# Graph layers on one core: edge passes by pairs of groups, with VectorE instructions of 1024 columns

## The reference

```python
for l in range(5):                                     # block 1, edge_attr_32
    h = leaky(x @ W1[l] + b1[l]) @ W2[l] + b2[l]
    e = leaky(edge_attr @ We1[l] + be1[l]) @ We2[l] + be2[l]
    msg = h[src] * e * dot_scale[l]
    agg = segment_sum(msg, dst, num_segments=n)
    x = layernorm(x + agg * res_w[l]) * ln_g[l] + ln_b[l]
# block 2: rst = segment_sum((features * deg_out**-0.5 @ weight)[src], dst) * deg_in**-0.5 + bias
# block 3: two transformer convolutions with a softmax over each target's edges
# block 4, edge_attr_64:
msgs = relu(node_inputs[src] + edge_inputs)
return node_inputs + segment_sum(msgs, dst, num_segments=n)
```

## Time and profile before

| | us |
|---|---|
| median of 3 runs | 7263.68 |
| the profiled execution | 7279.41 |
| its span | 7277.8 |
| PE busy | 5581.7 (77%) |
| VectorE (DVE) busy | 5235.6 (72%) |
| ScalarE (ACT) busy | 2933.9 (40%) |
| GpSimd (POOL) busy | 3154.9 (43%) |
| mean granted TensorE clock | 0.877 |

### The profile page before, as it was taken

The page is one execution under the profiler, slowest core; times in us unless marked ns, Lnnn a source line. Parts: engine busy times, 40 slices in busy tenths (PEclk is TensorE's granted clock), DMA queues, the critical chain, the costliest instruction groups (busy, mean ns, idle before and its releaser), DMA issues. The chain is left out here.

```text
span 7277.8 us, 277545 instructions
## 1 busy us (share of the span) xinstructions
PE 5581.7 (77%) x87504; PEld 4594.4 (63%) x87511; DVE 5235.6 (72%) x14769; ACT 2933.9 (40%) x5054; POOL 3154.9 (43%) x4856
## 2 busy tenths in 40 slices
PE   4888888855555467777777777776889998999777
PEld 3666666633444357677677677676857776777676
DVE  7555555568999968888788788788955554555698
ACT  2444444423444534334344343343833332333343
POOL 1777767648777535445355354453000000000254
PEclk9989889975555579999899899898969998999999
DMA  2666666632222368778688587685631111111497
GB/s 73 195 190 189 187 179 191 184 104 63 73 72 74 125 195 230 191 192 230 154 229 231 154 229 208 173 230 159 244 114 61 62 64 47 64 64 64 113 237 202
DMA packets 1403295, 1098.83 MB, mean 151 GB/s; under 512 B 1012405, under 2 KB 1171820, under 8 KB 1393466
## 3 DMA queue, kind: packets, MB, share of 16 engines
q1 hardware_dynamic: 787494, 772.05, 34.5%
q0 software_dynamic: 224768, 240.90, 13.7%
q10 hardware_dynamic: 390804, 82.65, 6.2%
HBM read 815.28 MB, written 278.78 MB: 150 GB/s over the span
## 5 line engine op out<-in xcount | busy, mean ns | idle before, releaser
L542 POOL DMA_DIRECT2D big<-rows x2592 | 1421.8, 549 | 3245.3 <-issue 2301.5
L1316 PE MATMUL ps<-big 128*128 128x64 bf16 x41472 | 1922.4, 194 | 619.4 <-DVE big L1818 223.7
L1316 PEld LDWEIGHTS ps<-big 128*128 128x128 fp8e4 x41472 | 1688.1, 98 | 698.5 <-issue 686.1
L1328 PE MATMUL ps<-big 128*128 128x64 bf16 x20736 | 1734.1, 194 | 11.2 <-issue 5.8
L811 POOL DMA_INDIRECT rows<-big x800 | 1038.1, 1298 | 529.0 <-issue 356.9
L1328 PEld LDWEIGHTS ps<-big 128*128 128x128 bf16 x20736 | 1069.9, 98 | 21.7 <-issue 13.8
L1607 DVE SCALAR_TENSOR_TENSOR big<-big 128x1000 f32<-128x1000 f32 (+1 forms) x300 | 359.6, 1199 | 664.2 <-ACT big L917 438.0
L1037 ACT CAST big<-big 128x512 bf16<-128x512 f32 x720 | 445.4, 619 | 902.2 <-DVE big L1831 901.4
L1276 PE MATMUL ps<-identb,big 128*128 128x128 bf16 x2304 | 441.8, 294 | 395.4 <-DVE big L1719 300.3
L1231 PEld LDWEIGHTS ps<-big 128*125 128x125 f32 (+1 forms) x4800 | 678.1, 210 | 101.1 <-issue 57.9
L1043 ACT CAST big<-big 128x512 bf16<-128x512 f32 x864 | 534.0, 618 | 455.8 <-issue 336.3
(11 more groups left out here) (264 smaller groups left out, 9442.8 us busy)
## 6 DMA issues: line engine op xcount, KB each, us to landing
big<-ohsD SPq DMA_DIRECT2D x432, 512.0 KB, 3.8
big<-ohdD SPq DMA_DIRECT2D x432, 320.0 KB, 4.3
big<-rows POOLq DMA_DIRECT2D x2592, 32.0 KB, 3.8
big<-rows SPq DMA_DIRECT2D x2592, 32.0 KB, 3.6
big<-maskD SPq DMA_DIRECT2D x50, 1600.0 KB, 6.7
big<-rows ACTq DMA_DIRECT2D x1728, 32.0 KB, 3.6
big<-keyT SPq DMA_DIRECT2D x100, 488.3 KB
maskD<-big SPq DMA_DIRECT2D x25, 1600.0 KB, 6.2
```

What stands on the lines that cost most here:

```text
L542: eng.dma_start(edge[:, s.r, j, :], rows[bass.ds(v[s.r * (hi - lo) + j - lo], P), col]).then_inc(landed[s.r], 16)
L1316: last = pe.matmul(pG[g.r][:, j * D:(j + 1) * D], ohsR[:, g.r, at:at + P].bitcast(F8), slices[:, g.r, q, (3 * k + c) * D:(3 * k + c + 1) * D],
L1328: last = pe.matmul(pacc[:, bass.ds(w[j], D)], hot[:, g.r, j * P:(j + 1) * P], parts[:, g.r, c, j * D:(j + 1) * D], start=False, stop=False ...
```

## The change

- Edge passes work on pairs of groups (`Pair` in place of `Step`, 72 pairs); the loop body holds four pairs (`PR`), that is 8 groups, and the rings are 8 groups deep.
- `message`, `rest` and `lower` are single instructions of 1024 columns. The parts are kept as f32, and TensorE and `rest`/`lower` read the upper two bytes of each f32 as a bf16 (`upper_half`, a view with a step of two elements). ScalarE's casts `upper` and `middle` go; in block 4 it applies the relu to the message in f32.
- The target one-hots are neither stored nor loaded; VectorE remakes all of them (`remake`, 2048 columns per pair) from the local ids. Four tiles' one-hots are interleaved (`[d, j]` with the tile innermost), against an iota that is spread four times (`iota4`). TensorE reads them with a step of four elements.
- In the counting stretch VectorE makes the source one-hots of four tiles in one instruction, two per group, and the target one-hots of all eight in one.
- ScalarE copies the table slices, and waits for the whole split of the table first. The shares of the edge tiles are 4 (SyncE), 3 (GpSimd) and 1 (ScalarE).

```diff
-G_LAG, S_LAG = 1, 5
 RING = 4
+PR = 4
+NPAIR = NG // 2
+PT = NPAIR // PR
+S_LAG = 3
...
+        iota4 = sb("iota4", [P, 2 * P, QUAD], BF16)
...
-        slices = carve(RING, 2, 6 * D, dt=BF16)
-        ohsR = carve(RING, 2 * GT * P, dt=U8)
-        edge = carve(RING, GT, D)
+        slices = carve(2 * PR, 2, 6 * D, dt=BF16)
+        ohsR = carve(2 * PR, 2 * GT * P, dt=U8)
+        edge = carve(2 * PR, GT, D)
...
-        SP_SHARE, POOL_SHARE, ACT_SHARE = (0, 3), (3, 6), (6, 8)
+        SP_SHARE, POOL_SHARE, ACT_SHARE = (0, 4), (4, 7), (7, 8)
...
+        def upper_half(v):
+            return v.bitcast(BF16).rearrange("p (a b) -> p a b", b=2)[:, :, 1]
...
+            def load_hots(u):
+                sp.dma_start(ohsR[:, 2 * u.r:2 * u.r + 2, :], ohsD[bass.ds(u.i * 2, 2)].rearrange("g p f -> p g f")).then_inc(ohs_loaded[u.r], 16)
...
+                def step(u):
+                    if u.r == 0:
                         hold(sp)
+                        v[:] = starts(SP, u.t, *SP_SHARE, 2 * PR)
+                    if u.live(PR):
+                        sp.wait_ge(m_ready, base + u.lag(PR).i + 1)
                         hold(sp)
+                    load_hots(u)
+                    load_edges(sp, v, u, *SP_SHARE, col, edge_loaded)
...
                 act.copy(tabp[1], tres).then_inc(tab_mid, 1)
+                act.wait_ge(tab_mid, nth + 1)
+                act.wait_ge(tab_lo, nth + 1)
+
+            def slice_tables(u, names):
+                for k in range(4):
+                    last = act.copy(slices[:, 2 * u.r + k // 2, k % 2, :], flat(tabq)[:, bass.ds(names[u.r * 4 + k], 6 * D)])
+                last.then_inc(sliced, 1)
...
+            def edge_pass(base, positive, col):
+                v = list(starts(SCALAR, 0, *ACT_SHARE, 2 * PR))
+                for r in range(PR):
+                    load_edges(act, v, Pair(0, r), *ACT_SHARE, col, edge_loaded)
+                names = list(tables_of(SCALAR, 0))
...
+            def scatter(u, k, j, at):
+                own = hot[:, u.r, (k * 2 + j // QUAD) * QUAD * P:(k * 2 + j // QUAD + 1) * QUAD * P].rearrange("p (d j) -> p j d", j=QUAD)
                 for c in range(3):
+                    f = k * GT * D + j * D
+                    last = pe.matmul(pacc[:, bass.ds(at, D)], own[:, j % QUAD, :], upper_half(part(u, c)[:, f:f + D]),
                                      start=False, stop=False, skip_group_check=True)
...
+            def turn_over(u, v, base, nth):
+                to = u.lag(S_LAG)
+                if u.live(S_LAG):
+                    pe.wait_ge(lo_ready, base + to.i + 1)
...
+                hold(pe)
+                w = halves(v[u.r * GT:(u.r + 1) * GT], (W - 1) * D) if u.live(S_LAG) else ()
...
+            def same(to, local, groups):
+                n = groups * GT // QUAD
+                return dve.tensor_tensor(to.rearrange("p (q d j) -> p q d j", q=n, j=QUAD),
+                                         iota4[:, 0:P, :].unsqueeze(1).to_broadcast([P, n, P, QUAD]),
+                                         local.rearrange("p (q j) -> p q j", j=QUAD).unsqueeze(2).to_broadcast([P, n, P, QUAD]), ALU.is_equal)
...
+            def src_hots(t, r, q):
+                dve.tensor_tensor(ohS[:, r % 2, q * QUAD * 2 * P:(q + 1) * QUAD * 2 * P].rearrange("p (i j) -> p i j", j=QUAD), iota4[:, :, :],
+                                  each(idm[:, r % 2, q * QUAD:(q + 1) * QUAD], 2 * P), ALU.is_equal).then_inc(hots_ready, 1)
...
                     if not past(i, NG - 1) or not isinstance(i, int):
-                        one_hots(*chunk(t, r, 1), m)
+                        if m == 0:
+                            dst_hots(*chunk(t, r, 1))
+                        if m in (1, QUAD):
+                            src_hots(*chunk(t, r, 1), m // QUAD)
...
+            def rest(u, base, kind):
+                if u.live():
...
+                    dve.tensor_tensor(part(u, 1), part(u, 0), upper_half(part(u, 0)), ALU.subtract).then_inc(res_ready, 1)
+
+            def lower(u, base):
+                if u.live(1):
+                    g = u.lag(1)
+                    dve.wait_ge(res_ready, base + g.i + 1)
+                    dve.tensor_tensor(part(g, 2), part(g, 1), upper_half(part(g, 1)), ALU.subtract).then_inc(lo_ready, 1)
+
+            def all_pairs(base, kind, nth):
+                def body(u):
+                    message(u, base, kind, nth)
+                    lower(u, base)
+                    remake(u)
+                    rest(u, base, kind)
+                steps(dve, body)
```

More of the change, by code:

```diff
@@ L728, in _ @@
+                    load_hots(u)
+                    load_edges(sp, v, u, *SP_SHARE, col, edge_loaded)
+                for r in range(PR):
+                    step(Pair(0, r))
+                with sp.Fori(1, PT) as t:
+                    for r in range(PR):
+                        step(Pair(t, r))
             with sp.Fori(0, LAYERS) as l:
@@ L1302, in open_sums, with gather @@
                     pe.matmul(bank(b), zerob[:, :], zerob[:, 0:1].to_broadcast([P, 512]), start=True, stop=False, skip_group_check=True)
[L1304 to L1314 removed]
+            def gather(u, k, j):
+                g, q = u.r * 2 + k, j // QUAD
+                for half in range(2):
+                    at = ((q * 2 + half) * QUAD + j % QUAD) * P
@@ L1326, in scatter @@
-            def scatter(g, j, w):
+                        last = pe.matmul(pG[g % 4][:, j * D:(j + 1) * D], ohsR[:, g, at:at + P].bitcast(F8),
+                                         slices[:, g, q, (3 * half + c) * D:(3 * half + c + 1) * D],
+                                         start=(half + c == 0), stop=(half + c == 3))
+                return last
+            def scatter(u, k, j, at):
+                own = hot[:, u.r, (k * 2 + j // QUAD) * QUAD * P:(k * 2 + j // QUAD + 1) * QUAD * P].rearrange("p (d j) -> p j d", j=QUAD)
@@ L1806, in _ @@
-            names = []
-            def slice_tables(s, base):
-                if s.live(0):
-                    if s.r == 0:
-                        hold(dve)
-                        names[:] = tables_of(DVE, s.t)
-                    if not s.known or s.i >= RING:
-                        dve.wait_ge(gathered, base + s.lag(RING).i + 1)
-                        hold(dve)
-                    for q in range(2):
-                        last = dve.tensor_copy(slices[:, s.r, q, :], flat(tabq)[:, bass.ds(names[s.r * 2 + q], 6 * D)])
-                    last.then_inc(sliced, 1)
@@ L1837, in rest, with remake @@
-            def rest(s, base, kind):
-                if s.live(3):
-                    g = s.lag(3)
-                    dve.wait_ge(hi_ready, base + g.i + 1)
-                    if not g.known or g.i >= 2:
-                        dve.wait_ge(lo_ready, base + g.lag(2).i + 1)
+                        dve.tensor_tensor(part(u, 0), got, own, ALU.mult).then_inc(m_ready, 1)
+                    else:
+                        dve.tensor_tensor(part(u, 1), got, own, ALU.add).then_inc(m_ready, 1)
+            def remake(u):
+                if u.live():
+                    same(hot[:, u.r, :], dstl[:, bass.ds(u.i * 2 * GT, 2 * GT)], 2)
@@ L1874, in _ @@
                 table_parts(l)
-                def body(s):
-                    slice_tables(s, l * NG)
-                    message(s, l * NG, "edge", l)
-                    rest(s, l * NG, "edge")
-                    lower(s, l * NG)
-                    remake(s, l * NG)
-                steps(dve, body)
+                all_pairs(l * NPAIR, "edge", l)
                 lc = Chain(dve, l_chain, l * END)
@@ L1895, in _ @@
             barrier(dve, "L0")
-            def plain_pass(base, kind):
-                def body(s):
-                    slice_tables(s, base)
-                    message(s, base, kind, LAYERS)
-                    rest(s, base, kind)
-                    lower(s, base)
-                    remake(s, base)
-                steps(dve, body)
             chain(dve.tensor_tensor(t2, x, over(deg[:, 0, :], D), ALU.mult))
```

355 lines of the change are left out of this document (124 added, 231 removed).

## The result

Seven runs of each kernel, taken in turn: 7317.93 us after (7306.15 to 7350.97), 7269.26 before (7249.06 to 7294.06). The ratio is 1.0084, with a 95% interval of 1.0065 to 1.0102: the change costs 47 to 74 us. The forecast was a gain of 15. The time lies inside the range of 7125 to 7510 that was given, on the other side of no change from the forecast, and 8 us above the 7190 to 7310 that belonged to the forecast itself. The profiled run of after took 7350.97 us, its span is 7349.4.

A forecast was written before the change was run, and what follows sets the result against it. SyncE's DMA issuing was taken to bound the edge passes. Edge passes -101, counting stretch +83 and spreading the iota +3 sum to -15 us, forecast 7249 us against the median of 7263.68, range 7125 to 7510.

The forecast's parts named there:

- the sum of the edge passes: Five layer passes 14 us earlier each, 70 us, and the last 31: -101 us, with bounds -200 and -10.
- the body of 8 groups: Edge passes: SyncE issues 8 groups in 23.45 us, 2.93 per group against 2.98; bounds 2.81 to 3.04.
- What bounds the passes: Layers' edge passes: SyncE's DMA issuing is the bound, its queue 98% full; DVE and PE wait for what it issues late.
- The start: Start of an edge pass: SyncE resumes 14.9 us after the table split, with 8 groups loaded ahead and not 4.
- The end: End of an edge pass: landing 3.7, late gather 0.4, DVE 5.9, PE 4.4 us, 14.4 until the sums are read.
- The last pass: Final edge pass: bodies of 21.8 us, sums read at 7225.7 against 7257.4, 31 us earlier.
- The wait that was to show it: Edge passes: the sign expected in the profile was DVE idle before the message, released by a DMA of rows.
- rival (a): Wide comparisons on DVE run at a column per cycle: 230 us more in counting, 20 in passes, time 7500; chance 0.12.
- rival (b): PE's strided reads in the edge passes are slow, 6.9 us a pair: +455 us, 7700; chance 0.12.
- rival (c): PE's longer loop body is fetched again at each of 102 returns: +255 us, 7505; chance 0.06.
- rival (d): Reading 32 values is nearly free and the counting stretch's small waits go: -200+63 us, 7127; chance 0.2.
- The counting stretch: Three 1024-column one-hots per group overrun gaps between dependent adds: 6.55 us a group against 5.97, +83 us; bounds +60, +310.

The follow-up runs named there:

- e1_pieces: The changed kernel with the counting stretch's one-hots cut into 8 pieces of 340 to 512 columns, one behind each add: 7203.71 us, ratio 0.9908 to the kernel before.

## Why the prediction was wrong, step by step

The step that failed is the sum of the edge passes, -101 us forecast and -18 measured: the body of 8 groups was sized too small, and the slow issuing at a pass's start stood in no term.

- **What bounds the passes: right.** SyncE's issuing, in both kernels. Taking 8 issues of 36 from it was worth 21 to 26 us a layer; giving the kernel before 4 more for 16 cost it 89.
- **The body of 8 groups: the mis-sized term.** Forecast 23.45 us, measured 24.02. The loop's end is 2.43 us and not 2.2 (the read 1.87 and not 1.75), a pair 5.37 to 5.48 and not 5.30. 0.57 is 2.4% of a body, but it stands 17 times in each of five passes, 48 us, and it turned the change's step from a gain of 0.39 into a loss of 0.18 a body. Where a queue is full and the change swaps one set of issues for another, the result is the small difference of two large sums, and rows good to 2% did not carry its sign. The forecast's bounds (2.81 to 3.04 us a group) held the measured 3.00; the value taken was too near the middle. More than half of the 0.57, 0.32 us, is the slower pace of issuing that both profiles of after have: at the pace of `e1_pieces` a pair takes 5.30 to 5.40 and the body 23.70, and what is left is mostly the loop's end (2.43 for 2.2). The rows that the prediction was made from have the faster pace.
- **The start: right, then a term that was missing.** SyncE resumes 14.2 us after the split (14.9 forecast). Then its first four sets of 8 issues take 5.2, 5.2, 5.0 and 6.6 us instead of 4.36, in the layers as in the last pass (4.91, 4.99, 6.17 instead of 3.95): about 5 us a pass beyond the bodies. What stretches them is open. In before the first sets of 6 after it resumes take 3.21, 3.22 and 3.37 us, no more than later ones, so no row had shown such a term, and the sum took all bodies at their even pace. SyncE's 68 pairs take 3579.85 - 3168.47 = 411.4 us; forecast 396.4.
- **The end** is 15.8 us and not 14.4. Per layer: 9.7 (bodies, of which 5.4 by the pace of issuing) + 5.3 (start) + 1.4 - 0.7 = 15.7 us more than forecast, which eats the 14. That is the difference between -70 and +1.
- **The last pass** came to -19 for -31. Its bodies nearly fit (21.96 us, forecast 21.8); SyncE resumes 1.2 us later than forecast, and the slow first sets and the end are most of the rest.
- **The wait that was to show it came at another place.** DVE was to idle for a DMA of rows. It idles 80.6 us for PE's gather, and PE 45.0 us for the load of one-hots: the same queue, but the first of its nine issues and not the last eight.
- **DVE at twice the rate, rival (a): right, and (a) fell.** 1024 columns take 0.68 us, 2048 take 1.22 and the next starts 1.13 later, and a pair takes DVE 4.54 us where 4.5 was forecast. This was read from the two-byte copy and agrees with the Trainium skill (VectorE: DVE Perf Modes, "The perf-mode tier table").
- **PE's strided reads, rival (b): fell.** Nine matmuls in 0.27 us, in steps of 4 elements for the weights. The rule of the Trainium skill (SBUF — State Buffer, "Specifications (TRN2)"), full speed from two hits on a 16-byte line on, holds in this trace. "PE 5.3 a pair" held as well: with SyncE out of the way PE and DVE give 5.4.
- **Code fetched again, rival (c): fell.** The code queue has 177 packets and 2.90 MB, 165 and 2.70: 12 packets more, for 102 returns.
- **The cheap read, rival (d): fell.** 32 values cost 1.87 us, and the small waits of the counting stretch stayed (6.53 us a group).
- **The counting stretch: right in its pattern, partly lucky in its size**, +79 for +83. By the text's own terms the large instructions cost 6.0 - 5.34 = 0.66 us a group, 95 us; the 6.55 that it went on with make 83. They measured 104, and the store that went, for which the sum had no term, gave 25 back. The two misses nearly cancel.
- **The sign.** +83 was nearly sure and -101 was a sum of small differences. I weighed them alike. The upper of the text's own bounds for the edge passes, -10, would have given +76 and the right side, and the chances (slower 0.37, faster 0.30) leaned that way already.

What stays open: what sets SyncE's pace of issuing, why a pair's gap before the next load is once 0.45 and else 0.38 us, and how much of the start's burst belongs to the transfers and how much to the reads. None of this was tried.

## What to carry to other kernels

Count the issuing queues as engines: the busy table leaves them out, and here the fullest of them set the pace, whatever was taken from the engines in the table. When work is moved to such a queue, look first for an engine with room (ScalarE had it, GpSimd had not), and price the loop's end with it. Long instructions are no gain inside a chain of short dependent ones, since the chain's gaps are a fixed size; cut the filler to the gap. And take several profiles before a difference in code that was not touched is explained, or a body is priced to 2%: even the pace of bare issuing differed by 1.6% between executions of one kernel (0.565 and 0.574 us).

## What the runs showed of the hardware

- A read of numbers from SBUF into an engine's registers grows almost in line with their count: 8 take 0.55 us and 16 take 1.02 on ScalarE, 24 take 1.42 and 32 take 1.87 on SyncE; on TensorE 8 take 0.59 and 32 take 2.14. The Trainium skill (DMA: Bandwidth & Descriptors, "Latency and other measured facts") gives a floor of some 600 ns for such a load. The rows of 8 values lie at it or just under (0.55 to 0.59), and each further value takes 0.05 to 0.065 us.
- DMAs of the same kind are issued 0.57 us apart by SyncE and 0.62 to 0.63 by GpSimd, in the layers' passes. SyncE's pace is not the same in every execution: 0.565 us in five profiles and 0.574 in nine, for one and the same code in both kernels, with GpSimd's at 0.631 in all of them.
- TensorE's mean granted clock in one stretch of unchanged code lay between 0.69 and 0.87 in four executions (two of each kernel), so the engine stood at its lower level (1.2 GHz, 0.50) for more or less of it, and the stretch took 311 to 358 us with that.
- Eight DMA issues of SyncE that take 4.36 us in the middle of a layer's pass take 5.0 to 6.6 us just after its start, in the changed kernel; six issues in before take no more there than later (3.21 to 3.37 us, and 3.37 to 3.39).
